# Where the value sums and the side pieces stand in TensorE's order: an attention kernel with a quantized feed-forward layer

## What is computed

```
q, k = l2_normalize(layernorm(x) @ w_q), l2_normalize(layernorm(x) @ w_k);  v = x @ w_v
resonance = 0.5 + 0.5 * tanh((q.k - 0.27) * 15)
fused = (resonance * gate_q * gate_k) @ v            # per head, over all 4096 keys
x1  = layernorm(x + fused @ w_o + b_o)
xq  = fp4_quant_dequant(x1)                          # blocks of 16
h   = silu(xq @ w_gate.T) * (xq @ w_up.T)            # width 704
out = layernorm(x1 + fp4_quant_dequant(h) @ w_down.T)
```

## Time and profile before

| what | value |
|---|---|
| median of 3 runs | 4381.3 us (4379.77 to 4382.84) |
| profiled execution, its own time | 4378.88 us |
| its span, first to last instruction | 4377.1 us |
| granted TensorE clock, mean | 0.995 of full speed |
| TensorE busy / ScalarE busy / VectorE busy | 94% / 92% / 36% of the span |
| ACTIVATEs of line 706 | 2816, from 307 us on |

### The profile page before, as it was taken

How to read it: one execution, slowest core, us unless ns; L and a number is a source line. 1 busy time by engine, 2 the same in 40 slices (tenths; PEclk the granted TensorE clock), 3 DMA queues, 4 the chain that set the end, 5 groups by cost and what they waited for, 6 DMA issues and landing times.

```text
span 4377.1 us, 69385 instructions
## 1 busy us (share of the span) xinstructions
PE 4111.8 (94%) x28776; PEld 1285.9 (29%) x28776; DVE 1561.6 (36%) x4540; ACT 4017.1 (92%) x3271; POOL 159.5 (4%) x120
## 2 busy tenths in 40 slices
PE   7988899999999999999999999999999999999997
PEld 5651222222222222222222222222222222222223
DVE  6754023333333332333233333333333333333236
ACT  4669999999999999999999999999999999999993
POOL 2330000000000000000000000000000000000001
PEclk9999999999999999999999999999999999999998
DMA  4454444344434443444334433443345334433450
GB/s 114 124 129 78 70 76 65 61 68 78 65 63 67 78 68 60 66 78 71 60 63 78 77 55 62 78 78 56 61 78 78 56 61 78 78 59 59 77 83 13
DMA packets 179871, 313.70 MB, mean 72 GB/s; under 512 B 65264, under 2 KB 141808, under 8 KB 154608
## 3 DMA queue, kind: packets, MB, share of 16 engines
q1 hardware_dynamic: 179568, 309.41, 42.1%
HBM read 266.82 MB, written 42.47 MB: 71 GB/s over the span
## 4 chain that ended last, share of the span: by engine, by line
PE 69%; ACT 23%; DVE 4%; issue 3%; DMA 1%; SPq 1%; POOL 0%; POOLq 0%; DVEq 0%; ACTq 0%
PE ps L1268 35%; ACT room L706 22%; PE ps L1258 20%; PE ps L1295 8%; PE ps L1318 4%; DMA m_f<-fused_t 1%; DVE room L858 1%; PE ps L1213 0%; DVE st L812 0%; DVE xnT L848 0%; PE ps L1224 0%; PE ps L1308 0%; DVE sm L773 0%; DVE sm L774 0%; DVE sm L775 0%
## 5 line engine op out<-in xcount | busy, mean ns | idle before, releaser
L706 ACT ACTIVATE room<-ps 128x1024 f32<-128x1024 f32 (+1 forms) x2816 | 3787.1, 1417 | 178.4 <-PE ps L1258 162.2
L1268 PE MATMUL ps<-room,vt 128*32 128x512 f32 x16384 | 2051.2, 601 | 0.0
L1258 PE MATMUL ps<-qs,room 64*128 64x512 f16 x8198 | 1325.9, 383 | 203.7 <-ACT room L706 182.6
L1258 PEld LDWEIGHTS ps<-qs,room 64*128 64x128 f16 x8198 | 310.4, 93 | 1749.5 <-ACT room L706 1123.1
L1268 PEld LDWEIGHTS ps<-room,vt 128*32 128x32 f32 x16384 | 388.1, 108 | 945.3 <-issue 945.3
L1295 PE MATMUL ps<-wguT,m_xqT 128*128 128x352 f32 x960 | 348.2, 485 | 0.0
L967 DVE TENSOR_TENSOR vz<-ps,vz 128x352 f32<-128x352 f32 x120 | 63.0, 525 | 757.7 <-ACT vz L716 757.7
L972 DVE TENSOR_TENSOR vz<-ps,vz 128x352 f32<-128x352 f32 x120 | 63.0, 525 | 595.9 <-PE ps L1295 595.9
L1318 PE MATMUL ps<-wdnT,wqk 128*128 128x256 f32 x720 | 198.9, 404 | 0.6 <-DVE wqk L937 0.6
L1295 PEld LDWEIGHTS ps<-wguT,m_xqT 128*128 128x128 f32 x960 | 162.6, 189 | 105.2 <-issue 54.3
L600 POOL TENSOR_TENSOR m_x<-m_x,bo 128x256 f32<-128x256 f32 x60 | 43.9, 731 | 3876.7 <-DMA m_x<-in_L_attn_x_dram 3876.7
(11 more groups left out here) (172 smaller groups left out, 2198.0 us busy)
## 6 DMA issues: line engine op xcount, KB each, us to landing
room<-k_parts SPq DMA_DIRECT2D x520, 256.0 KB, 9.4
vt<-v_gated SPq DMA_DIRECT2D x65, 1024.0 KB, 17.9
qs<-q_parts SPq DMA_DIRECT2D x520, 32.0 KB, 10.1
gqb<-q_gates SPq DMA_DIRECT2D x256, 64.0 KB, 2.2
room<-in_L_attn_x_dram SPq DMA_DIRECT2D x16, 512.0 KB, 4.1
v_gated<-vz SPq DMA_DIRECT2D x64, 128.0 KB, 2.2
fused_t<-fs SPq DMA_DIRECT2D x256, 32.0 KB, 1.7
q_parts<-room SPq DMA_DIRECT2D x30, 256.0 KB, 2.4
```

The source lines that it names most:

```text
L706: act.activation(res[:, c, o:o + m, :], ps[:, o:o + m, :], ACT.Sigmoid, scale=2 * SHARP / QK_UP ** 2, bias=-2 * SHARP * THRESH).then_inc(b ...
L1258: ins = pe.matmul(ps[:, BANK[n % 2] + i, :], ks[o:o + HROWS, par, h // 2, kt * P:(kt + 1) * P], qs[o:o + HROWS, par, h // 2, :], start=Tru ...
L1268: ins = pe.matmul(ps[32 * h:32 * h + 32, SUM_BANK, :], vt[:, par, n * HD:n * HD + 32], r, start=kt == 0, stop=kt == KT - 1, skip_group_che ...
```

## The change

Three tables are changed, and nothing else. The order of the 32 key tiles stays 0 to 31.

- `SUMS` replaces the formula in `sums_at`. Before, two key tiles stood behind the scores made in every fourth step (4, 8, ... 36, where four banks of scores are made), one in the step two later, and none in odd steps until the unit's end. Now most key tiles stand in odd steps, where two banks of scores are made: six steps (11, 15, 19, 27, 31, 35) have two tiles, twenty have one.
- `END` and `BEGIN`: H0, D0 and D1 and P and X come one step later, into even steps (H0 into an odd one); H1 stays; G0 to G3 come two steps later and stay in odd steps.
- `GATE_ACT`: the two sigmoids of the gate come two groups later, with G0 and G1.

```diff
+SUMS = {
+    1: [0], 3: [1], 4: [2], 5: [3], 6: [4], 7: [5], 9: [6], 11: [7, 8], 13: [9], 15: [10, 11],
...
+    [22, 23], 32: [24], 35: [25, 26], 36: [27], 39: [28], 40: [29], 42: [30], 43: [31]
+}
 def sums_at(g):
-
-    at = {0: [], 40: [29], 42: [30], 43: [31]}
-    for c in range(10):
-        if c:
-            at[4 * c] = [3 * c - 1, 3 * c]
-        at[4 * c + 2] = [0, 1] if c == 0 else [3 * c + 1]
-    return at.get(g, [])
+    return SUMS.get(g, [])
...
-BEGIN = {7: "P", 19: "X", 23: "G0", 27: "G1", 31: "G2", 35: "G3"}
-END = {0: "H0", 3: "H1", 11: "D0", 15: "D1"}
-GATE_ACT = {25: 0, 29: 1}
+BEGIN = {8: "P", 20: "X", 25: "G0", 29: "G1", 33: "G2", 37: "G3"}
+END = {1: "H0", 3: "H1", 12: "D0", 16: "D1"}
+GATE_ACT = {27: 0, 31: 1}
```

More of the change, by code:

```diff
@@ L61, with last_group @@
 NIN = 2 * 2 * len(PAIRS) + 1
-def sums_at(g):
-    at = {0: [], 40: [29], 42: [30], 43: [31]}
-    for c in range(10):
-        if c:
-            at[4 * c] = [3 * c - 1, 3 * c]
-        at[4 * c + 2] = [0, 1] if c == 0 else [3 * c + 1]
-    return at.get(g, [])
-assert sorted(k for g in range(NGRP) for k in sums_at(g)) == list(range(KT))
+SUMS = {
[3 rows of a table added]
+}
+def sums_at(g):
+    return SUMS.get(g, [])
+def last_group(n):
+    return max(g for g in range(NGRP) if FIRST[g] <= n)
+assert [k for g in sorted(SUMS) for k in SUMS[g]] == list(range(KT))
+assert all(last_group(KEY * HG + HG - 1) <= g <= last_group(KEY * HG) + 5 for g in SUMS for KEY in SUMS[g])
 FH = F // 2
-BEGIN = {7: "P", 19: "X", 23: "G0", 27: "G1", 31: "G2", 35: "G3"}
-END = {0: "H0", 3: "H1", 11: "D0", 15: "D1"}
-GATE_ACT = {25: 0, 29: 1}
+BEGIN = {8: "P", 20: "X", 25: "G0", 29: "G1", 33: "G2", 37: "G3"}
+END = {1: "H0", 3: "H1", 12: "D0", 16: "D1"}
+GATE_ACT = {27: 0, 31: 1}
 PREP = {3 + 4 * i: i for i in range(9)}
```

## The result

The changed kernel takes 4356.45 us (4354.47 to 4356.85, 4 runs) against 4380.58 (4379.77 to 4382.84, 4 runs): ratio 0.9943, 95% interval 0.9926 to 0.9960. Forecast was 4362. The profiled execution went from 4378.88 to 4356.28, its span from 4377.1 to 4354.5.

What follows compares the result with a forecast made beforehand. TensorE and ScalarE bound it, handing time to each other. Full units -23.7, units 1 and 3 -0.7, unit 2 +3.9, unit 0 +0.2, tail +0.8: -19.5 from 4378.9, median 2.4 higher, 4362; 8-in-10 range 4325 to 4388.

Steps and rivals of the forecast that it cites:

- ScalarE's and TensorE's prices and the walk: Start-to-start prices walked through a unit's 44 steps: 62.24 us before against 62.32 read; new order 61.24 if nothing else binds.
- TensorE's work would grow and its waits shrink by more: Full unit: TensorE's work 58.7 to 59.45, 0.75 us more; its waits 3.5 us before, 1.8 in the new order.
- The ring: Key tile 0 to G3 (52.40), G3 through VectorE's quantization to the end of `fs` (9.45): 61.85 us per unit, wait 0.61.
- Rival 1: The ring does not bind and the whole us per full unit comes: 4325 us; chance 0.14.
- The joins: Pieces behind four banks, H0 and H1 behind sums: extra cost taken as 0, at most 0.8 (six times 0.13).
- Rival 2: Slower: six pieces each pay 0.13 for their join within the ring: 4408 us, with half of that 4385; chance 0.12.
- the rule weighed in the prediction: Trainium skill: one matmul's drain overlaps the next's fill, so splitting pairs costs nothing; time about 30 us lower. Not followed.
- Unit 2: `PREP` pieces behind two tiles make the group of four wait 0.94, not 0.34: 64.7 against 60.8, +3.9.
- Unit 0: First unit, with its pieces in steps 9 to 17: +0.2 us.
- The tail: After the last unit, starting behind its `fs`: +0.8 us.
- Rival 3: It evens out: the ring comes 0.2 to 0.4 us longer than walked, 4373 to 4386 us; chance 0.14.

Runs made afterwards that it cites:

- e1: Changed kernel with one operation of width 704 left out of VectorE's quantization of the hidden tile (values not the reference's): 4326.4 us, full units 61.30.
- e2: Changed kernel with one operation of width 704 done twice in VectorE's quantization of the hidden tile: 4434.4 us.
- e3: Kernel before, with one operation of width 704 done twice in VectorE's quantization of the hidden tile: 4386.3 us, full units 62.33.
- e11: Changed kernel with G3 in step 36 and key tile 27 in step 37, in place of 37 and 36: 4324.08 us, 0.9870 of the kernel before.
- e7: Changed kernel, but units 0 and 2 keep the old table of key tiles: 4350.1 us.
- e4: Changed kernel with key tile 0 in step 2 and not in step 1: 4362.5 us, full units 61.81.
- e10: The changed kernel once more, unaltered, for a second profile of its tail: 4353.5 us, tail 86.6.
- e5: New table of key tiles with the old steps for the pieces and the gate sigmoids: 4846.6 us, full units 69.96.
- e8: e7 with other tables for the full units, found by walking many (G3 in step 36, H0 in 0): 4299.47 us, 0.9802 of the kernel before.

## Why the prediction was right, step by step

**ScalarE's and TensorE's prices and the walk.** Right. The prediction gives the walk by stretches, and three of the four are within 0.03 us; the first, which holds the ring's wait, is 0.12 shorter than forecast. That TensorE's work would grow and its waits shrink by more is borne out in kind, and was mis-sized: busy 60.35 in the window above against 59.83 in the earlier trace rows is 0.5 more and not 0.75, and its idle time in these windows went from 2.57 to 1.45. (The sum in the prediction has a slip: 60 times -0.39 is -23.4 and not -23.7, which changes nothing.)

**The ring.** Right in place and kind, mis-sized by 0.13 us. TensorE's part, from key tile 0 (2041.80 + 3.62) to G3 (56.05 into the unit), measured 52.43 against 52.40. The part from G3 to key tile 0 was put at 9.45 and measured 9.32: I let `fs` start 0.03 behind the end of the quantization, and it started 0.08 ahead of it. The wait was 0.45 and not 0.61. With the 0.08 by which the walk of the old order was short of what was read, the gain of a full unit was 0.57 and not 0.39 us; over 60 units that is 11 us more than forecast, of which unit 0, the tail and stage A took back 8. That the time came within 6 us of 4362 is owed in part to this: two misses of opposite sign, and only the first belongs to the mechanism. e1, e2, e3 and e11 show that it is this ring: 0.93 of VectorE costs 0.93, less costs less only down to 61.30, and moving G3 opens it. Rival 1, the whole us, was wrong only in thinking that nothing stood in its way; 61.30 is its unit, forecast 61.24, reached in e11.

**The joins.** Right, 0 within what the rows resolve. P, D0 and X behind four banks show 0.54 ahead of them and their old lengths; D1 takes 1.90 to the next sums (2067.45 to 2069.35) where D0 takes 1.81, the only place with something extra. Rival 2 had its six times 0.13 there, and is out. The rows of the new order also keep 0.99 for one tile and 1.85 for two, so a change of kind still costs 0.13, against the rule weighed in the prediction.

**Unit 2.** Right: 64.7 forecast, 64.55 measured, with the clock at 1.00 in both. The earlier trace rows had the piece's length, and e7 shows that its place behind pairs does it: 2.2 us came back, and 1.6 more would have but for the fall of the clock.

**Unit 0.** A term of the sum that failed: +0.2 forecast, +3.1 measured. The prediction asked only whether the unit's pieces are hidden, and put nothing down for TensorE's clock, which is at its lower level when the unit starts. Unit 0 of the kernel before, of the changed kernel, of e9 (the old order again) and of e4 (the new table but for key tile 0), then a stretch of the changed kernel's unit 0:

```profile
307.00:372.70 65.70, 53.88 (x408) 12.76 (x410) 32.76 (x76) 61.03 (x46) 6.00 (x2) 0.92 0.48 88
...
307.70:376.50 68.80, 56.72 (x412) 12.41 (x410) 32.77 (x76) 60.91 (x47) 6.00 (x2) 0.90 0.47 84
...
310.10:378.30 68.20, 56.40 (x408) 13.15 (x410) 32.75 (x76) 61.14 (x46) 6.00 (x2) 0.88 0.46 85
...
307.50:373.60 66.10, 54.81 (x412) 12.23 (x410) 32.76 (x76) 60.59 (x46) 6.01 (x2) 0.92 0.48 87
...
321.90:328.70 6.80, 5.77 (x26) 0.90 (x28) 0.00 (x0) 4.79 (x4) 0.00 (x0) 0.50 0.03 6
```

The clock rises early in the unit, and in some executions it then falls a second time, as in the last row. Where it does for 6.8 us, the unit takes 68.22 with the old table (e9) and 68.5 to 69.0 with the new one (the changed kernel, e10, e1, e2, e5), and with half of that 67.44 (e11); where it does not, 65.5 to 65.8 with the old table and 66.15 in e4. So most of the 3.1 us is the second fall, and the order's own share is some 0.4. The fall came in six of seven profiled executions of the new table in this unit and in one of six of the old one: that the new order brings it on is likely, and not shown. e7, whose clock did not fall again, decides nothing about the pieces.

**The tail.** +0.8 forecast, +5.5 in the profile; the part of it that can be traced to the order is 1.0. H0 of the last tile starts 2.94 behind the last group's start before, in both profiles, and 3.93 after, in both. The rest differs between executions. The windows of two tails, the kernel before and the changed one, the stretch behind H0 and H1 (granted clock 0.69 and 0.61):

```profile
4297.70:4315.00 17.30, 8.93 (x26) 5.42 (x26) 11.60 (x55) 1.41 (x4) 1.92 (x3) 0.69 0.15 42
```

```profile
4270.50:4289.40 18.90, 10.54 (x26) 6.34 (x26) 11.60 (x55) 1.42 (x4) 1.93 (x3) 0.61 0.13 37
```

The same 26 matmuls took 1.6 us longer at a mean clock of 0.61 of full speed than at 0.69. In the repeats this stretch took 17.3 (before, 0.67) and 17.2 (after, 0.72), and the tails 87.8 and 86.6 us; e11's took 84.7. No run isolates what the clock follows in the tail; that the order moves it by more than 1 us is not shown.

**The chances.** 0.60 for the forecast, whose own range was 4350 to 4373: it came at 4356. Rival 3, an even outcome, would have needed the ring longer than walked; it was shorter.

## What to carry to other kernels

When two engines hand work to each other step by step, measure start-to-start prices in the rows and walk the order by hand: it gave every full unit here within 0.2% (but for the falls of the clock in e2), also orders 12% slower, and found one 2% faster. Then look for the ring that closes over the end of the loop: take the longest chain on an engine that seems idle (here 7.2 us of quantization and what queues behind it), and compare its end with the first step of the next round that needs it, since a shift of two groups turned 2.45 us of cover into a wait. And check the odd rounds, by their granted clock too: a table tuned for the 60 full units cost 3.8 us in unit 2, and units with more idle time are where the clock fell in e4, e7 and e8.

## What the runs showed of the hardware that I had not expected

A short wait can cost more than itself. In e2 TensorE waits 1.31 us for `fs` in each of 59 units; in 18 of them its clock fell to 1.2 GHz for some 3 us, from 0.1 to 1.3 us behind the end of the wait, and the unit grew by 1.1 to 1.6 us more. The other 41 waits are as long and had no such fall; what decides between them no run shows. Two such places of e2, by the timeline of TensorE, the first fallen and the second not:

```profile
751.33 1.43 PE L1278 MATMUL ps<-room,vt 128*32 128x512 f32 x8 [1.31 <-DVE fs L992]
752.69 1.12 PE L1314 MATMUL ps<-idf,xh 128*128 128x128 f32 x4
...
815.27 1.07 PE L1278 MATMUL ps<-room,vt 128*32 128x512 f32 x8 [1.30 <-DVE fs L992]
816.26 0.66 PE L1314 MATMUL ps<-idf,xh 128*128 128x128 f32 x4
```

and the granted clock by windows there:

```profile
748.00:754.00 6.00, 4.38 (x28) 1.21 (x22) 3.37 (x5) 4.26 (x4) 0.00 (x0) 0.83 0.10 22
754.00:762.00 8.00, 7.88 (x60) 1.56 (x56) 1.01 (x3) 7.18 (x5) 0.73 (x1) 0.92 0.93 156
...
812.00:820.00 8.00, 5.99 (x50) 1.47 (x43) 4.32 (x7) 6.70 (x6) 0.00 (x0) 1.00 0.11 28
```

Ahead of both TensorE did the same and was idle 0.31 and then 1.3 us. The changed kernel, with 0.31 and 0.38, keeps 61.75 or 61.76 in each of its full units. The Trainium skill (TensorE: Matmul & The Clock Gate, section HAM oscillation — how this bites in real kernels) gives as the rule to avoid much longer gaps; here the clock fell behind 1.3 us, with a shorter gap just ahead, in 18 of 58 units, and behind 0.31 and 1.38 in light units of e4 and e7.

VectorE started an operation ahead of the end of the one before where the kernel makes it wait for nothing: `fs` started 0.08 us before the quantization's last operation ended, in every full unit of the changed kernel. The quantization's own operations, each of which waits by a semaphore for the one before, start 0.03 us behind its end.
